# A two-layer convolution on one core: layer 0's last eight units stay in SBUF, the statistics loads are spread anew, and the mid-unit wait is split by block

## What is computed

```python
def _gn(v, G=4, eps=1e-5):
    B_, C_, H_, W_ = v.shape
    g = v.reshape(B_, G, C_ // G, H_, W_)
    m = jnp.mean(g, axis=(2, 3, 4), keepdims=True)
    s = jnp.var(g, axis=(2, 3, 4), keepdims=True)
    return ((g - m) / jnp.sqrt(s + eps)).reshape(v.shape)

x = x + _L0_conv_ref(_gn(x), L0_conv_weight, L0_conv_bias)   # 3x3, pad 1, 8 -> 8 channels
x = x + _L1_conv_ref(_gn(x), L1_conv_weight, L1_conv_bias)
```

## Time and profile before

| | before |
|---|---|
| median of three runs | 3852.91 us |
| the profiled execution | 3844.09 us, its span 3842.5 us |
| TensorE busy | 90% |
| VectorE, ScalarE, GpSimd busy | 36%, 45%, 16% |
| packets of the DMA queues, share of 16 engines | 41.4% (ScalarE's loads), 35.8% (stores), 18.6% (statistics) |
| DRAM read, written | 805 MB, 537 MB |
| mean granted TensorE clock | 0.978 |

### The profile page before, as it was taken

The page is one execution under the profiler, slowest core; times in us unless marked ns, Lnnn a source line. Parts: engine busy times, 40 slices in busy tenths (PEclk is TensorE's granted clock), DMA queues, the critical chain, the costliest instruction groups (busy, mean ns, idle before and its releaser), DMA issues. The chain is left out here.

```text
span 3842.5 us, 215729 instructions
## 1 busy us (share of the span) xinstructions
PE 3470.0 (90%) x98528; PEld 1826.4 (48%) x98528; DVE 1388.6 (36%) x2370; ACT 1736.7 (45%) x1586; POOL 596.5 (16%) x1098
## 2 busy tenths in 40 slices
PE   0698999999899998999989999898998989999998
PEld 0354545455444554544445444454544445455554
DVE  7454224542245321553225532255222552223200
ACT  0344444444444444444444444444444444444454
POOL 0111111111111111111111111111111111111111
PEclk9999999999999999999999999999999999999999
DMA  9699999999989998999989999899998999999898
GB/s 348 236 383 326 405 380 336 373 326 405 361 333 363 339 418 306 384 350 363 407 306 390 335 371 399 296 390 335 384 403 298 386 331 396 385 286 310 272 310 269
DMA packets 334151, 1344.28 MB, mean 350 GB/s; under 512 B 38832, under 2 KB 38960, under 8 KB 301232
## 3 DMA queue, kind: packets, MB, share of 16 engines
q10 hardware_dynamic: 149680, 537.61, 41.4%
q0 software_dynamic: 147456, 536.94, 35.8%
q1 hardware_dynamic: 36864, 268.45, 18.6%
HBM read 805.45 MB, written 536.87 MB: 349 GB/s over the span
## 5 line engine op out<-in xcount | busy, mean ns | idle before, releaser
L446 PE MATMUL conv<-x_tile,wts 32*32 32x512 f32 x49152 | 3387.7, 601 | 139.8 <-issue 24.6
L451 PE MATMUL conv<-x_tile,wts 32*32 32x512 f32 x49152 | 3408.1, 603 | 0.0
L446 PEld LDWEIGHTS conv<-x_tile,wts 32*32 32x32 f32 x49152 | 1596.1, 103 | 1694.0 <-issue 1358.8
L361 ACT ACTIVATE out_tile<-conv,bias 128x1024 f32<-128x1024 f32 x512 | 570.8, 1115 | 1891.6 <-PE conv L451 1859.7
L451 PEld LDWEIGHTS conv<-x_tile,wts 32*32 32x32 f32 x49152 | 955.8, 103 | 73.8
L510 DVE BATCH_NORM_STATS2 bn_mid<-out_tile 128x6 f32<-128x512 f32 x960 | 617.5, 685 | 901.2 <-ACT out_tile L361 665.0
L502 DVE BATCH_NORM_STATS2 bn_x<-stat_tile 128x6 f32<-128x512 f32 x912 | 561.9, 679 | 969.4 <-DMA stat_tile<-x_dram 969.2
L365 ACT ACTIVATE out_tile<-conv,bias 64x1024 f32<-64x1024 f32 x512 | 567.1, 1108 | 26.7 <-DVE bn_mid L523 13.2
L367 ACT ACTIVATE out_tile<-conv,bias 64x1024 f32<-64x1024 f32 x512 | 569.1, 1112 | 13.2
L260 POOL DMA_DIRECT2D mid_dram<-out_tile x512 | 273.0, 533 | 1520.8 <-ACT out_tile L361 1021.1
L260 POOL DMA_DIRECT2D out_dram<-out_tile x512 | 268.1, 524 | 1521.6 <-ACT out_tile L361 1049.7
(11 more groups left out here) (60 smaller groups left out, 148.0 us busy)
## 6 DMA issues: line engine op xcount, KB each, us to landing
stat_tile<-x_dram SPq DMA_DIRECT2D x256, 1024.0 KB, 9.7
mid_dram<-out_tile POOLq DMA_DIRECT2D x512, 512.0 KB, 9.0
out_dram<-out_tile POOLq DMA_DIRECT2D x512, 512.0 KB, 9.1
x_tile<-x_dram ACTq DMA_DIRECT2D x504, 512.0 KB, 12.3
x_tile<-mid_dram ACTq DMA_DIRECT2D x504, 512.0 KB, 12.2
x_tile<-x_dram ACTq DMA_DIRECT2D x8, 480.0 KB, 6.9
x_tile<-mid_dram ACTq DMA_DIRECT2D x8, 480.0 KB, 6.2
x_tile<-pad_row ACTq DMA_DIRECT2D x16, 32.0 KB
```

The costliest lines, as they stand in the source:

```text
L361: act.activation(out_tile[:, slot, 0], conv[:, parity, 0], ACT.Identity, bias=bias[:, 0:1]).then_inc(evicted, 1)
L446: nc.tensor.matmul(columns_of(parity, i, q, c), wts[part, MAIN, kw], rows_of(TILE * q, TILE, slot, c, kw), start=first, stop=end)
L451: last = nc.tensor.matmul(columns_of(parity, i, q, 1 - c), wts[part, ABOVE, kw], rows_of(TILE * above, TILE, slot if q else (slot - 1) % S ...
```

## The change

Units 24 to 31 of layer 0 are evicted into a new tile `keep` and are not stored to DRAM. Layer 1 gets blocks 47 to 62 from `keep`, by DMA from SBUF to SBUF. A block is shifted by one row against the results, so it comes in two parts from two places: the last row of it (8 partitions, 32 KB) by `load_last_row`, issued at the unit at which the whole block was issued before, and the other 15 rows (120 partitions, 480 KB) by `load_kept`, issued one unit later, after a wait for the former. Each of the two signals a semaphore of its own. Block 47 takes its 15 rows from `mid_dram`, block 63 needs no last row. The statistics loads are spread anew: six of them come before units 24 to 30, where nothing is stored, and ten instead of sixteen in layer 1. The wait at mid-unit is split in two: the second half of a block's columns waits for the first half of the same block.

```diff
+KEPT = 8
+KEPT_FROM = UNITS - KEPT
+KEPT_ROWS = range(2 * KEPT_FROM - 1, BLOCKS - 1)
+TURNS = (2 * UNITS - KEPT) // RING
...
-STAT_UNITS = (list(range(0, 24, 2)) + 4 * [UNITS] +
-              [35, 36, 38, 39, 41, 42, 44, 45, 47, 48, 50, 51, 53, 54, 56, 57])
+STAT_UNITS = (list(range(0, 24, 2)) + [24, 25, 26, 27, 28, 30] + 4 * [UNITS] +
+              [36, 38, 41, 43, 46, 48, 51, 53, 55, 57])
...
+        keep = sb("keep", [P, KEPT, 2, SIDE])
...
-                    for i in range(2):
-                        store(n, g, i)
+                    if not is_kept(g):
+                        for i in range(2):
+                            store(n, g, i)
...
+            def load_kept(n, b):
+
+                if b < 2 * KEPT_FROM:
+                    rows = rows_of(1, n, ROWS * b + 1, ROWS - 1)
+                else:
+                    rows = keep[CH:P, b // 2 - KEPT_FROM, b % 2]
+                act.dma_start(x_tile[0:P - CH, b % SLOTS, 1:SIDE + 1], rows) \
+                   .then_inc(rows_loaded[b % SLOTS], 16)
+
+            def load_last_row(b):
+                act.dma_start(x_tile[P - CH:P, b % SLOTS, 1:SIDE + 1],
+                              keep[0:CH, (b + 1) // 2 - KEPT_FROM, (b + 1) % 2]) \
+                   .then_inc(last_row_loaded, 16)
+
+            def kept_rows_at(g):
+                blocks = (2 * (g + TRIP - 1 - UNITS) + 1, 2 * (g + TRIP - UNITS))
+                return [b for b in blocks if b in KEPT_ROWS]
...
+                for b in kept_rows_at(g - 1):
+                    if b == kept_rows_at(g - 1)[0]:
+                        through = kept_rows_at(g - 1)[-1] - KEPT_ROWS[0] + 1
+                        act.wait_ge(last_row_loaded, 16 * len(KEPT_ROWS) * n + 16 * through)
+                        act.sem_inc(rows_asked)
+                    load_kept(n, b)
...
-                    if at // UNITS < 2:
+                    if at // UNITS == 1 and 2 * (at % UNITS) + of in KEPT_ROWS:
+                        load_last_row(2 * (at % UNITS) + of)
+                    elif at // UNITS == 1 and 2 * (at % UNITS) + of == BLOCKS - 1:
+                        load_kept(n, BLOCKS - 1)
+                    elif at // UNITS < 2:
                         load_block(at // UNITS, n, 2 * (at % UNITS) + of)
...
+                to = keep[:, g - KEPT_FROM] if is_kept(g) else out_tile[:, g % RING]
...
-            def add(parity, j, c, kw):
+            def add(parity, j, i, c, kw):
...
                 for kw in range(KW):
-                    last = add(parity, j, 0, kw)
-                last.then_inc(half_added, 1)
-                pe.wait_ge(half_added, UNITS * p + TRIP * t + (j + 1))
-                pe.sem_inc(unit_begun)
+                    for i in range(2):
+                        last = add(parity, j, i, 0, kw)
+                        if kw == KW - 1:
+                            last.then_inc(half_added[i], 1)
                 for kw in range(KW):
-                    last = add(parity, j, 1, kw)
+                    for i in range(2):
+                        if kw == 0:
+                            pe.wait_ge(half_added[i], UNITS * p + TRIP * t + (j + 1))
+                            pe.sem_inc(unit_begun)
+                        last = add(parity, j, i, 1, kw)
                 last.then_inc(conv_done, 1)
```

More of the change, by code:

```diff
@@ L41 @@
 RING = 4
+KEPT = 8
+KEPT_FROM = UNITS - KEPT
+KEPT_ROWS = range(2 * KEPT_FROM - 1, BLOCKS - 1)
+TURNS = (2 * UNITS - KEPT) // RING
+assert KEPT % RING == 0
 EVICTS = 3
@@ L147, in conv_preact_blocks @@
         rows_wanted, rows_asked = sem("rows_wanted"), sem("rows_asked")
-        half_added, conv_done = sem("half_added"), sem("conv_done")
+        half_added = [sem(f"half_added{i}") for i in range(2)]
+        conv_done = sem("conv_done")
         second_taken = sem("second_taken")
@@ L167, in stores_before, with is_kept @@
         def stores_before(n, g):
-            return 32 * (2 * UNITS // RING * n + g // RING)
+            turn = g // RING if g < UNITS else (g - KEPT) // RING
+            return 32 * (TURNS * n + (min(turn, KEPT_FROM // RING) if g < UNITS else turn))
+        def is_kept(g):
+            return KEPT_FROM <= g < UNITS
         def evicts_through(n, g, parts):
@@ L352, in evict @@
                 layer, u = divmod(g, UNITS)
-                slot, parity = g % RING, g % 2
+                parity = g % 2
+                to = keep[:, g - KEPT_FROM] if is_kept(g) else out_tile[:, g % RING]
+                slot = g % RING
                 act.wait_ge(conv_done, units_through(n, g))
-                if g >= RING or not first_image:
+                if (g >= RING or not first_image) and not is_kept(g):
                     act.wait_ge(stored[slot], stores_before(n, g))
-                if layer == 0 and u >= RING:
+                if layer == 0 and RING <= u < KEPT_FROM:
                     act.wait_ge(mid_taken, UNITS * n + (u - RING + 1))
                 if layer == 1 and u < RING:
-                    act.wait_ge(mid_taken, UNITS * n + (UNITS + u - RING + 1))
-                act.activation(out_tile[:, slot, 0], conv[:, parity, 0], ACT.Identity,
+                    act.wait_ge(mid_taken, UNITS * n + (KEPT_FROM + u - RING + 1))
+                act.activation(to[:, 0], conv[:, parity, 0], ACT.Identity,
                                bias=bias[:, 0:1]).then_inc(evicted, 1)
@@ L438, in columns_of @@
                 return conv[column:column + TILE, parity, i, c * BANK:(c + 1) * BANK]
-            def add(parity, j, c, kw):
+            def add(parity, j, i, c, kw):
                 first, end = c == 0 and kw == 0, c == 1 and kw == KW - 1
[L442 to L454, removed]
+                slot = 2 * j + i
+                for q in range(QUARTERS):
+                    part = slice(TILE * q, TILE * (q + 1))
+                    nc.tensor.matmul(columns_of(parity, i, q, c), wts[part, MAIN, kw],
+                                     rows_of(TILE * q, TILE, slot, c, kw), start=first, stop=end)
+                for q in range(QUARTERS):
+                    above = (q - 1) % QUARTERS
+                    part = slice(TILE * above, TILE * (above + 1))
+                    last = nc.tensor.matmul(columns_of(parity, i, q, 1 - c), wts[part, ABOVE, kw],
+                                            rows_of(TILE * above, TILE,
+                                                    slot if q else (slot - 1) % SLOTS, 1 - c, kw),
+                                            start=first, stop=end)
                 return last
@@ L506, in take_mid @@
             def take_mid(n, u):
+                of = keep[:, u - KEPT_FROM] if is_kept(u) else out_tile[:, u % RING]
                 for i in range(2):
```

7 lines of the change are left out of this document (4 added, 3 removed).

## The result

The changed kernel takes 4056.69 us (median, 4052.46 to 4058.83) against 3852.18 us for the kernel before in the same session: 5.2% slower, ratio 1.052 (95% interval 1.051 to 1.054). The forecast was 3843 us, and its range ended at 3912. The profiled execution took 4056.24 us, its span is 4054.6 us, 212.1 us more than before.

The account below looks back on a forecast made before the run. DMA was taken to pace layer 0 under statistics, TensorE everything else. Images 0 to 6 sum to -3.5 us, the last to -6.3: together -10 from 3844.1, 3834; plus 8.8 gives 3843 us, range 3803 to 3912.

Parts of the forecast that it names:

- The wait by block: TensorE's mid-unit wait: 0.13 us less per unit where TensorE sets the pace, 8.3 us in the last image.
- Statistics stalls in layer 1: Layer 1 with ten statistics loads instead of 16 would lose its 3.7 us of stalls per image.
- Statistics at the end of layer 0: Layer 0, units 24 to 31: added statistics loads cost nothing; the faster wait gains 0.9 us per image.
- VectorE at the layer's end: End of layer 0: later statistics use up VectorE's idle time and cost 2.3 us in each of seven images.
- The moves: End of layer 1: two-part moves from SBUF cost 6.0 us per image, 2.0 in the last.
- the rival with chance 0.30: Layer 1's end paced by the ring of moves, rounds about 7.6 and 10.1 us: 3890 us, chance 0.30.
- Issuing: Term of the round of moves on ScalarE's queue: 0.3 us.
- The landing behind it: Landing within the round of moves in layer 1; whole round 7.0 us, bounds 5.6 and 8.3, without statistics.
- The engine time: DMA engine time in the round of moves: 1.34 us per large move, as for a store.
- those have several us to spare: Layer 1's end: next moves and next unit's evictions behind ScalarE's wait were claimed to have several us to spare.
- a slack of 1.0 us: Layer 1's large moves: 5.9 us of lead against an urgent block's landing of 4.9 leave 1.0 us.
- B: Rival formed after the measurement, for layer 1's end: moving from SBUF is itself the cost; no size or chance given.

Follow-up runs that it names:

- e1: Kernel before with only the mid-unit wait split by block: 3831 us, ratio 0.992 to 0.996.
- e10: Kernel before with the wait by block and the changed kernel's statistics places, all stored and loaded from DRAM: 3897 us.
- e2: Changed kernel with the statistics loads at their places of before: 4056 us.
- e12: Changed kernel with only the 480 KB moves, in the original turn, no last rows or wait, statistics places of before: 3896 us.
- e6: Kernel before with the wait by block, all stored; blocks 47 to 62 loaded from DRAM in the changed kernel's two parts, order and wait: 3989 us.
- e3: Changed kernel with the 32 KB pair issued ahead of the wait and of the 480 KB pair: 4030 us.
- e4: Changed kernel without the 32 KB loads and their wait, the 480 KB moves issued at the original turn: 3918 us.
- e8: Changed kernel without the 32 KB loads and their wait, the 480 KB moves still one unit late: 3960 us.
- e9: Changed kernel, complete, with both parts of a block issued at the original turn and no wait between them: 3955 us.
- e7: Changed kernel with the 32 KB moves issued by SyncE at the same units, ScalarE still waiting for them: 3992 us.
- e13: Changed kernel, both parts in the original turn without wait, and two of layer 1's sixteen statistics loads moved to layer 0's units 24 and 26: 3910 us.

## Why the prediction was wrong, step by step

- **The wait by block: right.** 0.12 to 0.13 us per unit, and 205.4 us for each layer of the last image (forecast: 209.1 less 4.1). It pays only where TensorE sets the pace, as said: under statistics layer 0's distances 1 to 24 stay. In medians e1 gains 20 us (its ratio's interval ends at 0.996), in profiled spans 8.6 (3842.5 to 3833.9), which is what the layers without statistics and their neighbours explain; the profiled execution of before is faster than all its timed runs, and that of e1 the slowest of four. I can't place the difference of 11 us.
- **Statistics stalls in layer 1: right.** The first 22 distances run at 6.6 us, and e10 shows the whole layer at 205.3: -7.5 for a forecast of -7.9.
- **Statistics at the end of layer 0: wrong in kind, +7.6 us per image for -0.9.** "2.1 MB, no more than the last layers ask for without trouble" compared bytes of different work. The last layers move half loads, half stores; here nothing is stored. In the window of loads alone 276 GB/s are moved while TensorE is held up for a load; at that rate 2.1 MB take 7.6 us, and the unit can't keep 6.6. By queue (below), a load costs 0.587 x 12 / 1.81 = 3.9 us per MB there, against 2.6 in the middle of layer 1. That contrast isn't all due to the missing stores: the loads here read `x_dram`, and those beside stores cost 0.453 x 90 / 13.95 = 2.9 in the middle of layer 0 before. A backlog has its part too: the two loads issued from 1778.43, while the stores of the middle still ran, had a median landing of 19.5 us. More than half of the 7.6 us is one unit, which takes 11.9 us on average for 6.7 before. e2, e12 and e10 show that the statistics loads make it; how it divides into ceiling, source and backlog is not shown.

```profile
q10 hardware_dynamic: 493, 1.81, 58.7%
q1 hardware_dynamic: 210, 1.46, 41.8%
```

- **VectorE at the layer's end: right, a little less.** +1.5 us for +2.3 (the sum itself, 1749.9 - 1747.70, gives 2.2). The timeline of image 3 shows the set between the two late turns; the last of these starts at 1833.86, 1.2 us after its unit's first eviction at 1832.68.

```profile
1825.85 3.39 DVE L577 BATCH_NORM_AGGREGATE mv_mid<-bn_mid 128x2 f32<-128x720 f32 x1
1829.15 2.42 DVE L572 BATCH_NORM_STATS2 bn_mid<-conv 128x6 f32<-128x512 f32 x4
1831.49 2.46 DVE L550 BATCH_NORM_STATS2 bn_x<-stat_tile 128x6 f32<-128x512 f32 x4
1833.86 2.47 DVE L572 BATCH_NORM_STATS2 bn_mid<-conv 128x6 f32<-128x512 f32 x4
```

- **The moves: the step that failed most.** The mechanism was the rival with chance 0.30 (the ring paces layer 1's end), but neither its size (7 us in the last image, 12 under statistics) nor the range held it: 22 and 27 us over TensorE's pace (81.5 and 86.2 against 59.6). Three terms of the round were mis-sized. Issuing: I allowed 0.3 us, taken from loads; four issues out of `keep` took 6.1 us in the round shown (e6, from DRAM, is 7.6 us better in the last image). The landing behind it: I set the whole round at 7.0 us, but in that round 5.5 pass after the last issue has ended, and the five rounds average 9.75. The engine time, the least of them: I took a store's 1.34 us per move; 480 KB at 2.97 to 3.75 us per MB are 1.5 to 1.8.
- **What was left out.** ScalarE's evictions stand behind the wait and behind the issues; "those have several us to spare" held for rounds of 7 us, not of 10. And the padding's wait at the layer's end lengthens behind fuller queues: from 2.6 to 7.7 us in the last image, and from 4.4 to 11.9 in layer 0 of image 3 in e10. The wait was in the trace of before and not in my sum. And the lead of one unit, which I gave a slack of 1.0 us for a landing of 4.9, is too short once ScalarE issues the small pair beside the large one: in e3 TensorE waits for large moves although ScalarE waits for nothing.

The rule of the Trainium skill ("DMA: Bandwidth & Descriptors", section "Queues, rings and completion order"), by which a DMA's increment comes after the earlier writes of the same DMA engine, agrees with the round shown: the large move issued at 3994.12 landed 8.9 us later, at 4003.0, and the small pair reported at 4004.90. It is not proved by it. Two rounds before, the order was the other way: the small pair issued from 3977.82 had let ScalarE go on by 3983.76, and the large move issued ahead of it at 3976.10 landed after 8.2 us, at 3984.3. The same section says that completion is not in the order of issue for one issuing engine, because a small DMA can run on fewer DMA engines than a large one, and the second case agrees with that. So the rule doesn't make a small pair wait for the whole of a large one.

Summed up by the last image, whose end has no statistics to confuse it, in us over TensorE's pace. The first column has the six distances among the moves, the second the two around the padding's wait; one more distance makes up the rest:

| | among the moves | at the padding | all nine |
|---|---|---|---|
| e4, large alone, in turn | 0 | 0 | 0 |
| e8, large alone, late | 0 | 0 | 0.5 |
| e9, both parts, in turn, no wait | 3.7 | -1.3 | 3.4 |
| e7, late, wait, small ones on SyncE | 1.9 | 8.7 | 10.6 |
| e6, late, wait, all from DRAM | 12.3 | 1.8 | 14.3 |
| e3, late, small first, wait passes at once | 15.3 | 6.5 | 22.8 |
| after | 17.1 | 3.9 | 21.9 |

No single cause stands alone. Restoring the lead and dropping the wait takes nearly all away (e9); so does moving the small issues to SyncE, the padding apart (e7); dropping only the wait's effect does not (e3). The loss needs the late large pair together with the small moves in ScalarE's queue; in the changed kernel it shows as a ring closed by ScalarE's wait. The source SBUF adds some 5 to 8 us of the 22 (e6 against after). B is not excluded for the 65 us of e12, but not separated there from the shape of the moves. A unit near distance 23 of layer 1 takes 12 to 14 us in image 3 of e12 and e13 (8.2 in e1). The record narrows it down: statistics loads stand before both of units 53 and 54 there, and with 53 and 55 instead this distance takes 6.6 us on average in e4. e6, all from DRAM, has 13.3 with the former. Why these loads beside the moves cost so much stays open, and so does how the 27 us under statistics divide.

## What to carry to other kernels

A wait on the queue that issues the loads turns independent transfers into a ring: count every issue of the round at the duration that its own kind has, the landing after the last one, and all that stands behind the wait. A ceiling in GB/s belongs to the mix of reads and writes from which it was read; when the change takes the stores away, it must not be carried over. And keeping data in SBUF saved nothing on the loads here, where the way back into place is by DMA: the move took the engines at least as long per MB as the load that it replaced. A run that takes a wait off the path can leave the time as it was, so look at what TensorE waits for in it before the wait is called the cause.

## What the hardware showed that I had not expected

- The issue of a move out of SBUF by ScalarE took a median of 0.86 us for 120 partitions (up to 2.65) and 1.6 for 8 (up to 3.9) in the changed kernel; the same shapes from DRAM in e6 took 0.34 (up to 1.6) and 0.31 (up to 2.2).
- Loads almost alone were served at 276 GB/s while TensorE waited for one; beside stores, where DMA held TensorE up, it was 383 in e10.
- ScalarE's queue cost 2.97 us per MB of all engines with moves from SBUF (e12) and 2.94 with loads from DRAM (e1) under statistics, 3.75 (e4) and 3.43 (e1) without.
- A 32 KB transfer of padding that ScalarE waits for held its next issue back 2.6 us in the last layer 1 before, 7.7 in the changed kernel, and 11.9 in layer 0 of e10.
- Where TensorE waited much, at the end of the last layer 1, its granted clock averaged 0.91 over 60 us, so some of the time ran at the lower of its two levels (1.2 GHz).
